# Layer 1 score lookups over twelve blocks, expert weight units on ScalarE and GpSimd, and two alternating PSUM banks in the aggregation

## What is computed

```python
def gat_layer(x, W, a_src, a_dst, bias, src, dst, heads, out_c, concat):
    h = (x @ W).reshape(n, heads, out_c)
    al_s = jnp.einsum('nhc,hc->nh', h, a_src)
    al_d = jnp.einsum('nhc,hc->nh', h, a_dst)
    e = jax.nn.leaky_relu(al_s[src] + al_d[dst], NEG_SLOPE)
    ex = jnp.exp(e - jax.ops.segment_max(e, dst, num_segments=n)[dst])
    z = jax.ops.segment_sum(ex, dst, num_segments=n)
    out = jax.ops.segment_sum(h[src] * (ex / (z[dst] + 1e-16))[:, :, None], dst, num_segments=n)
...
W1 = wf1 + mg1 * ws1 + hf1          # experts: fast + gate * slow + hebb, for both matrices
h = jnp.square(jnp.maximum(flat_x @ W1 + bb1, 0.0))
y = h @ (wf2 + mg2 * ws2 + hf2) + bb2
```

## Time and profile before

| | us |
|---|---|
| median of 3 runs | 3213.5 |
| lowest and highest of them | 3208.41, 3224.72 |
| the profiled execution, its own time | 3225.58 |
| span of the profiled execution | 3223.8 |
| PE, DVE, ACT, POOL busy | 1833.6, 1385.2, 772.8, 1391.2 |
| DMA moved | 580.89 MB, mean 180 GB/s |

### The profile page before, as it was taken

One profiled execution on the slowest core, in us unless ns is written; L12 is line 12 of the kernel. 1 busy time (PEld: TensorE's weight loads), 2 busy tenths in 40 slices (PEclk: granted clock), 3 DMA queues, 4 the chain that ended last, 5 costly groups with the idle time before them and its releaser, 6 DMA issues. The chain is left out here.

```text
span 3223.8 us, 50021 instructions
## 1 busy us (share of the span) xinstructions
PE 1833.6 (57%) x14982; PEld 1228.4 (38%) x14983; DVE 1385.2 (43%) x2368; ACT 772.8 (24%) x2073; POOL 1391.2 (43%) x1323
## 2 busy tenths in 40 slices
PE   4578874056555655363679315555554474199980
PEld 3444552033333333232345203333333274177760
DVE  7656556555556556593763330000000185011115
ACT  3201100023333333351012003333332321033330
POOL 0355563266667767343000035555555433412216
PEclk9788886556666667676899655656666655599995
DMA  4311110168778778423327768888888683145449
GB/s 142 85 32 47 32 27 17 61 221 255 249 248 258 250 248 253 154 60 87 102 66 245 239 224 269 274 268 270 270 270 271 218 315 126 32 160 166 157 147 395
DMA packets 182781, 580.89 MB, mean 180 GB/s; under 512 B 49268, under 2 KB 51315, under 8 KB 182473
## 3 DMA queue, kind: packets, MB, share of 16 engines
q0 software_dynamic: 81744, 351.62, 34.7%
q1 hardware_dynamic: 75790, 159.71, 15.0%
q10 hardware_dynamic: 25200, 69.03, 5.6%
HBM read 473.74 MB, written 106.49 MB: 180 GB/s over the span
## 5 line engine op out<-in xcount | busy, mean ns | idle before, releaser
L1314 PE MATMUL acc<-ring,work 128*32 128x192 f32 x3904 | 350.7, 493 | 310.1 <-ACT work L1376 197.1
L1230 POOL DMA_INDIRECT ring<-feat_tab,islot x392 | 419.4, 1070 | 236.5 <-issue 108.8
L1269 DVE TENSOR_TENSOR work<-iota_f,dst_rel 128x224 f32<-128x224 f32 x112 | 44.1, 394 | 701.8 <-PE acc L1314 328.4
L639 POOL DMA_INDIRECT work<-score_tab,islot x224 | 230.7, 1030 | 168.8 <-DVE islot L692 102.0
L1314 PEld LDWEIGHTS acc<-ring,work 128*32 128x32 f32 x3904 | 147.8, 143 | 377.8 <-issue 341.2
L1314 PE MATMUL acc<-work 128*32 128x192 f32 (+1 forms) x2208 | 198.3, 461 | 162.4 <-ACT work L1376 111.1
L1380 ACT ACTIVATE work<-work 32x192 f32<-32x192 f32 x800 | 287.6, 360 | 10.7
L1230 POOL DMA_INDIRECT work<-feat_tab,islot x224 | 234.5, 1047 | 127.4 <-issue 54.3
L596 PE MATMUL acc<-wg,work 128*128 128x384 f32 x600 | 225.8, 527 | 30.2 <-issue 28.1
L1314 PE MATMUL acc<-big,work 128*32 128x192 f32 x1744 | 168.7, 475 | 120.1 <-ACT work L1376 87.2
L1230 POOL DMA_INDIRECT big<-feat_tab,islot x168 | 179.4, 1068 | 97.5 <-issue 41.0
(11 more groups left out here) (351 smaller groups left out, 3270.8 us busy)
## 6 DMA issues: line engine op xcount, KB each, us to landing
slot_out<-ring SPq DMA_DIRECT2D x57, 384.0 KB, 2.3
agg_raw<-work ACTq DMA_DIRECT2D x50, 388.0 KB
ring<-agg_raw SPq DMA_DIRECT2D x50, 388.0 KB
feat_tab<-work ACTq DMA_DIRECT2D x50, 384.0 KB
ring<-lo_rows SPq DMA_DIRECT2D x49, 256.0 KB
edges<-in_w_fast SPq DMA_DIRECT2D x28, 384.0 KB
edges<-in_w_slow SPq DMA_DIRECT2D x28, 384.0 KB
edges<-in_w_hebb SPq DMA_DIRECT2D x28, 384.0 KB
```

The lines of the kernel that those rows point to most:

```text
L639: pool.indirect_dma_start(sg[:, h, k * H:(k + 1) * H], None, score_tab[0], bass.IndirectOffsetOnAxis(ap=islot[:, h * 8 + k:h * 8 + k + 1], ...
L1230: pool.indirect_dma_start(rows[k][:, 0:C], None, feat_tab[l], bass.IndirectOffsetOnAxis(ap=islot[:, h * UN + k:h * UN + k + 1], axis=0)).t ...
L1269: ins = V.tensor_tensor(out, near.to_broadcast([P, BATCH, WIN]), dst_rel[:, cols].unsqueeze(2).to_broadcast([P, BATCH, WIN]), ALU.is_equal)
L1314: m = nc.tensor.matmul(sums_ps[c * WIN:(c + 1) * WIN, 0:n], hot, row[:, c * CHUNK:c * CHUNK + n], start=start, stop=True, skip_group_check ...
```

## The change

In `products_scores` the lookups go 4 to a block over 12 blocks, ahead of chunks 1, 2, 4 and 5; the low bits have 8 buffers; the expert weight units have four buffer sets (the fourth lies in `xn` and `tmp`); their scaling is done by ACT in four copies with a scale, their two additions by POOL; SP's stores and loads of units stand among the loads of low bits. ACT does one unit a block in the first 12 blocks and the other 16 in blocks 12 to 23. In `aggregate` the windows go to two PSUM banks in turn; PE picks the bank by a register and a branch for every call of `sums`; there are two `onehot_x`; ACT copies straight from PSUM to the row buffer in five copies and releases the bank behind the fifth; `stage` and its copy are gone. PE's scheduled steps after the lookups move with `LOOK_BLOCKS`. The core of the diff:

```diff
-GPB = 7
+GPB = 4
 LOOK_BLOCKS = GROUPS // GPB
+LO = 2 * GPB
+US = 4
...
-            unit_parts = [[spot(C) for _ in range(3)] for _ in range(2)]
-            lo_b = [spot_r(GT * P // 2).bitcast(bf16) for _ in range(GPB)]
+            unit_parts = [[spot(C) for _ in range(3)] for _ in range(3)] + [[xn[0], xn[1], tmp[0]]]
+            lo_b = [spot_r(GT * P // 2).bitcast(bf16) for _ in range(LO)]
...
+                    def added(j, h, n):
+                        fast, slow, hebb = unit_parts[h]
+                        pool.wait_ge(scaled, j + 1)
+                        pool.wait_ge(unit_in[h], n * 48 + 48)
+                        pool.sem_inc(tick_p, 1)
+                        nc.gpsimd.tensor_tensor(slow, slow, hebb, ALU.add).then_inc(unit_tmp, 1)
+                        pool.wait_ge(unit_tmp, j + 1)
+                        pool.sem_inc(tick_p, 1)
+                        nc.gpsimd.tensor_tensor(fast, fast, slow, ALU.add).then_inc(unit_done, 1)
+                    before = 4
+                    with pool.Fori(0, before) as i:
+                        for h in range(US):
+                            added(i * US + h, h, i)
                     pool.wait_ge(ex_st, 16)
...
+                    def swap(j, h, n):
+                        store(j, h)
+                        load(j + US, h, n + 1)
+                    turns = GROUPS // (2 * LO)
+                    with sp.Fori(0, turns - 1) as i:
+                        for g in range(2 * LO):
+                            sp.wait_ge(pick_ready, i * (2 * LO) + (g + 1))
+                            low_bits(i * (2 * LO) + (g + LO), g % LO)
+                            if g % 4 == 3:
+                                swap(i * US + g // 4, g // 4, i)
                     sp.wait_ge(first_st, 16 * NB)
...
+                    turn_of = {1: 0, 2: 1, 4: 2, 5: 3}
                     with pe.Fori(0, LOOK_BLOCKS // 2) as i:
-                        with_lookups(i * 2, 0, i * (2 * GPB), 0)
-                        with_lookups(i * 2 + 1, 1, i * (2 * GPB) + GPB, GPB)
-                    with_lookups(LOOK_BLOCKS - 1, 0, (LOOK_BLOCKS - 1) * GPB, 0)
+                        for j in range(2):
+                            products(i * 2 + j, j, lambda k: lookup(i * LO + (j * GPB + turn_of[k]), turn_of[k] % 2) if k in turn_of else None)
+                    lookup(GROUPS - 1, 0)
...
+                    def scale(j, h, n):
+                        slow = unit_parts[h][1]
+                        act.wait_ge(unit_in[h], n * 48 + 48)
+                        act.sem_inc(tick_a, 1)
+                        for a in range(4):
+                            part = slow[:, a * (C // 4):(a + 1) * (C // 4)]
+                            ins = nc.scalar.activation(part, part, ACT.Copy, scale=scales[:, ds(j * 4 + a, 1)])
+                        ins.then_inc(scaled, 1)
...
-                    with dve.Fori(0, UNITS // 2) as i:
-                        st.loop(i, 4)
-                        for h in range(2):
-                            combined(i * 2 + h, h, i)
...
+                    def place(bank, c, a, z):
+                        return acc[c * WIN:(c + 1) * WIN, bank, a:z]
+                    def opened(b, k, t, j):
+                        pe.wait_ge(open_ready, b)
+                        pe.wait_ge(flushed, b)
+                        sums(onehot_x[j], k, t, True, j).then_inc(open_mm, 1)
...
-                            sums(onehot[:, k, :], k, t, False).then_inc(tile_mm, 1)
+                            bank = pe.snap(bank_reg, min_val=0, max_val=BANKS - 1)
+                            with pe.If(bank > 0):
+                                added(i, k, t, 1)
+                            with pe.Else():
+                                added(i, k, t, 0)
...
                                 with pe.Fori(b0 + 1, b1 + 1) as b:
-                                    pe.wait_ge(open_ready, b)
-                                    pe.wait_ge(flushed, b)
-                                    sums(onehot_x, k, t, True).then_inc(open_mm, 1)
+                                    pe.reg_mov(bank_reg, b & (BANKS - 1))
+                                    bank = pe.snap(bank_reg, min_val=0, max_val=BANKS - 1)
+                                    with pe.If(bank > 0):
+                                        opened(b, k, t, 1)
+                                    with pe.Else():
+                                        opened(b, k, t, 0)
...
+                    act.sem_inc(flushed, BANKS - 1)
...
                             act.wait_ge(closed, q + 1)
-                            nc.scalar.activation(stage[w % 2], sums_ps, ACT.Copy).then_inc(flushed, 1)
-                            next_hot(q + 2)
-                            act.wait_ge(flushed, q + 1)
                             for c in range(4):
                                 nc.scalar.activation(raw[sl][w * WIN:(w + 1) * WIN, c * CHUNK:(c + 1) * CHUNK],
-                                                     stage[w % 2][c * WIN:(c + 1) * WIN, 0:CHUNK], ACT.Copy)
-                            m = nc.scalar.activation(raw[sl][w * WIN:(w + 1) * WIN, C:ROW],
-                                                     stage[w % 2][zp:zp + WIN, CHUNK:CHUNK + ZC], ACT.Copy)
-                            m.then_inc(blk_ready, 1)
+                                                     acc[c * WIN:(c + 1) * WIN, w % BANKS, 0:CHUNK], ACT.Copy)
+                            nc.scalar.activation(raw[sl][w * WIN:(w + 1) * WIN, C:ROW],
+                                                 acc[zp:zp + WIN, w % BANKS, CHUNK:CHUNK + ZC], ACT.Copy).then_inc(flushed, 1)
+                            next_hot(q + 3, (w + 3) % 2)
```

179 lines of the change are left out of this document (89 added, 90 removed).

## The result

The changed kernel takes 3172.2 us (median of 4 runs, 3159.4 to 3180.5) where the kernel before took 3218.1 beside it: ratio 0.987, interval [0.983, 0.991]. It is faster, but by 46 us where 210 were forecast, and outside the range. The profiled run took 3168.4 (span 3166.6).

A forecast was written before the change was run, and what follows sets the result against it. Taken as bounds: DVE, PE, then waiting for unit pieces in products_scores; PE waiting for ACT to empty the bank in the aggregations. Savings of 100 + 77 + 33 = 210 us off 3213.5 gave 3004 us, range 2900 to 3120.

The forecast's parts named there:

- Lookups: In products_scores: the 49 groups keep their DVE work, POOL's additions cost 16 us, so the first scan comes at 1673.
- a hold of 12 us stays hidden: SP's order in products_scores: waiting 12 us on a unit swap delays no low bits, as 8 buffers cover 24 us.
- the collisions: In the lookups: POOL's 24 additions slow DVE's operations through shared ports, 16 us in all, least 0, most 49.
- The stalls kept at 22: Two stalls of 9.45 and 12.68 us in the first loop turn of products_scores, with loads in flight, assumed to stay.
- Products and units: In products_scores after the first scan: 13 product blocks take 101 us, units stay hidden under PE, part ends 1790 to 1793.
- Aggregation: Both layers: removing PE's wait for ACT, less the cost of choosing banks, saves 77 us in layer 1, 33 in layer 0.
- a window of 6.48 less the 2.52 of waiting for ACT: Aggregation, layer 1: without PE's wait a window takes 3.96 us, with 1.5 us of bank choices 5.4.
- three limits: Aggregation, layer 1, per window: PE 5.4, POOL 4.85, transfers 5.3 us; overlapping with loss, 5.7 us was taken.
- the step from 6.56 to 6.2 us: Aggregation, layer 0: window time falls to 6.2 us, taken between PE's 6.6 and POOL's 5.7, saving 33 us.
- The choice of bank: PE's register and branch in each of 491 calls of `sums` per layer: 0.30 us a call, ends 0.08 and 0.57.
- Rival (a): Only lookups and units gain; the aggregation keeps its pace through other limits or the bank choices' cost: 3114 us, chance 0.18.
- Rival (c): Aggregation: PE fetches its doubled loop body anew at each of 56 turns, costing 529 us: 3643 us, chance 0.06.

## Why the prediction was wrong, step by step

**Lookups: mis-sized.** The first scan was forecast 191 us behind the part's start and came after 1715.3 - 1485.8 = 229.5. The failed step is "with 8 buffers (24 us of groups) a hold of 12 us stays hidden": the hold ahead of the last group was 17 us of waiting for POOL, and SP, held behind unit swaps, cost DVE 24.5 us of waits for low bits in all instead of 2.2. Next, the collisions came to (676 - 489 + 694 - 359) x 49 = 25.6 us, not 16, within the bounds given (0 to 49). The stalls kept at 22 were 25.9, but under a wrong name: they were not loads but PE's signals, late while POOL issued its stores, and one line in the kernel before removes them.

**Products and units: right in kind.** PE kept pace with 12 blocks in the lookups, DVE had no operation on units, and the units stayed hidden; ACT's four scalings took 442 ns each, not 359, and POOL's additions 1.84 us, not 2.04, without effect on when the units were done. The end came 6 us behind PE's last matmul instead of 12. What I did not have was the 10.4 us in which PE waits for the exponentials: I had moved the units into SP's order and did not ask what stood behind them. From the first scan to the end were 127 us instead of 118. Together 52 instead of 100.

**Aggregation: the step that failed most** is "a window of 6.48 less the 2.52 of waiting for ACT (252.4 / 100) leaves 3.96". The wait is real, but ACT's 0.34 us was never what filled it: 2.3 us of the 2.52 lie between the end of PE's closing matmul and the start of ACT's copy. With the wait gone and no choice added, a layer gains 25 us, not 250. None of the three limits that I set (PE 5.4, POOL 4.85, transfers 5.3) was reached: without the choice layer 1 stays at 6.3 us a window, with half of PE's columns too, and with it at 6.5. A slip besides: for layer 0 the step from 6.56 to 6.2 us is worth 0.36 x 99 = 36 us and not 33, which changes nothing here.

**The choice of bank** cost 0.08 us a call in layer 0 and 0.04 in layer 1, below my 0.30 (which of the branch's 77 and 215 ns belongs to the taken one no row shows; that was my guess). But it stood against a gain of 0.05 a call, not of 0.5. Bank and choice together were a loss of 16 us in layer 0 and a gain of 3 to 10 in layer 1, where I had forecast gains of 33 and 77. Rival (a), that the aggregation keeps its pace because the emptying was only where another limit showed, is what happened, with the first part's gain halved; I gave it 0.18.

**Rival (c)** did not happen (23 packets of code in the whole run), as argued, but one matmul more in each call brings it in layer 0.

**Still open:** why PE's signals are late on one kind of chip and not on the other, and what exactly holds the aggregation at 629 us without the choice. That indirect DMAs on POOL have to do with it is shown in the lookups, by spreading them; in the aggregation, where they can't be left out, it is only argued from the timelines and from the two chips.

## What to carry to other kernels

A wait that the profile puts down to an engine is only worth its length if that engine's own instruction fills it: compare the end of the releasing instruction with the start of the waiting one (here 0.34 us of copy under 2.5 us of wait), and look at what that engine was itself waiting for (here 262.9 us of "remote"). A per-call branch on PE has to be set against what is gained per call, not per window, and a queue that gets new waits (SP here) has to be read for what stands behind each of them. The best kernel of this study keeps the first half of the change, the old single bank, low bits and exponentials early in SP's order and the 25 stores spread: 0.969 [0.965, 0.973] of the kernel before, against 0.987 of the change.

## What the hardware showed that I had not expected

- The same kernel (the one before) takes 2873 us on one chip and 3180 to 3218 on others. The difference is nearly all in three parts with indirect gathers: `transform` 330 against 403 to 431, the old aggregation 592 against 666 us in layer 0 and 510 against 653 in layer 1; `scores`, `experts` and the feature parts agree within 2%.
- On the slower kind, a signal of PE can reach ACT or DVE 5 to 9 us after the modelled end of the instruction while POOL issues indirect DMAs in a row (2004.31 to 2009.18, 1503.10 to 1512.32), 2.3 us in the median of layer 1's windows; on the other it takes 0.1 us.
- A branch for each call of `sums` took PE's granted clock from 0.66 to 0.50 (1.2 GHz throughout) in layer 0 with no other work changed. Where there is no choice, layer 1's time did not follow the clock: 653 us at 0.66 and 650 at 0.50, 629 at 0.74 and 630 at 0.50, with half the columns at 0.50 each time.
- The changed kernel's loop body goes round without its code being fetched again (23 packets of code in the whole run); one instruction pair more in each call brought 244 packets more, and 12.4 us a turn in layer 0.
